# Two transformer layers on one core: weight splits, routing chain, first keys and last batch rearranged

## The reference

```python
x = layernorm(x + latent_attention(x))     # 16 heads, causal, rank 192 queries, rank 64 keys and values
x = layernorm(x + experts(x))              # 16 experts of 256-128-256, the best 2 for each token
x = layernorm(x + attention(x, Wq, Wk, Wv, Wo, bo))  # 16 query heads, 4 key heads, rotary, alibi, 30*tanh(s/30)
x = layernorm(x + x @ binarised(weight).T + bias)
```

## Time and profile before

| | |
|---|---|
| median of 3 executions | 567.59 us |
| the profiled execution, its own time | 566.75 us |
| its span, first to last instruction | 564.9 us |
| mean granted TensorE clock | 0.957 |
| TensorE busy | 508.0 us, 90% |
| VectorE busy | 394.8 us, 70% |
| ScalarE busy | 337.0 us, 60% |
| GpSimd busy | 308.7 us, 55% |
| chain that ended last, by engine | PE 68%, DVE 10%, ACT 6%, issue 5%, DMA 5%, POOL 4% |

### The profile page before, as it was taken

The page is one execution under the profiler, slowest core; times in us unless marked ns, Lnnn a source line. Parts: engine busy times, 40 slices in busy tenths (PEclk is TensorE's granted clock), DMA queues, the critical chain, the costliest instruction groups (busy, mean ns, idle before and its releaser), DMA issues.

```text
span 564.9 us, 10664 instructions
## 1 busy us (share of the span) xinstructions
PE 508.0 (90%) x3547; PEld 438.8 (78%) x3570; DVE 394.8 (70%) x840; ACT 337.0 (60%) x755; POOL 308.7 (55%) x300
## 2 busy tenths in 40 slices
PE   8889999999996995699993798999999999999982
PEld 7568888888874884486772587999999899999882
DVE  2678888888872165749753688778866995578464
ACT  5546677777765244253340587768766866686552
POOL 4846777677763024639753168766544644466210
PEclk9999999999998997789996899999999999999996
DMA  8939999900000921243575000000000000000011
GB/s 279 391 113 372 305 323 316 313 13 0 0 0 1 368 116 56 82 128 106 160 253 209 23 0 2 1 1 1 2 2 0 1 1 2 2 1 2 1 38 39
DMA packets 17582, 56.80 MB, mean 101 GB/s; under 512 B 2580, under 2 KB 12314, under 8 KB 15738
## 3 DMA queue, kind: packets, MB, share of 16 engines
q1 hardware_dynamic: 14784, 49.81, 26.0%
q0 software_dynamic: 2752, 6.40, 3.2%
HBM read 49.19 MB, written 28.45 MB: 137 GB/s over the span
## 4 chain that ended last, share of the span: by engine, by line
PE 68%; DVE 10%; ACT 6%; issue 5%; DMA 5%; POOL 4%; SPq 1%; ACTq 0%; DVEq 0%; POOLq 0%
PE bank L435 10%; PE bank L437 8%; PE bank L436 8%; PE bank L483 5%; PE bank L525 4%; PE bank L544 3%; PE bank L906 3%; PE bank L527 2%; PE bank L668 2%; PE bank L653 2%; PE bank L655 2%; PE bank L654 2%; PE bank L555 2%; DMA wqk_raw<-in_wqk 2%; PE bank L923 2%
## 5 line engine op out<-in xcount | busy, mean ns | idle before, releaser
L999 ACT ACTIVATE probs<-bank,neg_max,q_scale 128x256 f32<-128x256 f32 (+1 forms) x128 | 63.7, 507 | 39.4 <-DVE neg_max L1565 39.4
L1775 POOL TENSOR_TENSOR probs<-probs,inv_sum 128x512 f32<-128x512 f32 x64 | 51.6, 827 | 44.0 <-DVE inv_sum L1573 44.0
L1808 POOL TENSOR_TENSOR exps<-exps,tables 128x256 f32<-128x256 f32 x32 | 25.2, 787 | 77.0 <-ACT exps L1092 77.0
L1795 POOL TENSOR_TENSOR swapped<-swapped,tables 128x512 f32<-128x512 f32 x32 | 42.9, 1339 | 24.0 <-ACT swapped L1030 23.8
L1092 ACT ACTIVATE exps<-bank 128x768 f32<-128x768 f32 x32 | 25.9, 810 | 42.2 <-PE bank L635 42.2
L1405 DVE TENSOR_TENSOR q_lo<-q_sum,q_hi 128x512 fp32r<-128x512 f32 x32 | 28.0, 877 | 28.4 <-ACT q_hi L1063 28.3
L1551 DVE TENSOR_TENSOR swapped<-bank,tables 32x512 f32<-32x512 f32 x64 | 44.4, 693 | 1.4
L1767 POOL TENSOR_TENSOR qT<-qT,swapped 128x512 f32<-128x512 f32 x32 | 40.8, 1274 | 7.1 <-DVE swapped L1551 7.1
L1911 POOL DMA_INDIRECT y_rows<-y_slot,dest x31 | 30.1, 972 | 23.7 <-DVE y_slot L1743 13.8
L435 PE MATMUL bank<-x,wq_hi 128*128 128x256 f32 x128 | 39.1, 306 | 2.7 <-DVE q_sum L1392 2.6
L525 PE MATMUL bank<-keysT,qT 128*128 128x256 f32 x128 | 38.3, 381 | 0.7 <-ACT wo_full L1214 0.7
(11 more groups left out here) (264 smaller groups left out, 1801.3 us busy)
## 6 DMA issues: line engine op xcount, KB each, us to landing
slots<-in_c_unused SPq DMA_DIRECT2D x20, 1036.0 KB, 36.9
gu_all<-in_gate_up SPq DMA_DIRECT2D x4, 1024.0 KB, 8.1
xg<-slots SPq DMA_DIRECT2D x31, 129.5 KB, 2.2
wvo_raw<-in_wvo SPq DMA_DIRECT2D x1, 2560.0 KB, 21.1
dn_all<-in_down SPq DMA_DIRECT2D x1, 2048.0 KB, 8.4
wq_full<-in_Wq SPq DMA_DIRECT2D x1, 2048.0 KB, 15.7
wo_raw<-in_Wo SPq DMA_DIRECT2D x1, 2048.0 KB, 10.7
yg<-y_rows SPq DMA_DIRECT2D x4, 512.0 KB, 5.2
```

What stands on the lines that cost most here:

```text
L999: ins = act.activation(probs[:, par, h, c0:c1], bank[:, 2 * par + h, c0:c1], ACT.Exp, bias=neg_max[:, par, i:i + 1], scale=q_scale[:, b, t ...
L1775: ins = pool.tensor_tensor(some, some, inv, ALU.mult)
L1795: pool.tensor_tensor(sw, sw, sin_rows(), ALU.mult).then_inc(at1["sin_done"], 1)
```

## The change

- Routing: marks are summed by TensorE in PSUM, onto the region addresses, in place of two VectorE steps; the index and slot casts and the address step are gone. In batch 3 the two tiles are added and measured apart. The sum of variance and epsilon is left to ScalarE's bias input. 14 filler matmuls stand ahead of the last transposes.
- Splits: all eight high parts ahead of the blocks on ScalarE; key, value and four query parts on VectorE, four on GpSimd. The routing weights come after them. `gated` and `act_tok` share memory with `swapped`; `y_slot` has six buffers. SP reads the block's register ahead of its wait. The filler rows have eight kinds.
- Layer 1: keys and values of both halves ahead of the first scores; ScalarE loads the Tanh table after the first swaps; the first bias rows move from step 1 to step 7 on GpSimd, the sine of the second keys from step 1 to step 0. In the last two steps ScalarE copies the context ahead of Exp.
- Last batch: output, norm, transposes, products and statistics by tile; the bias is added by TensorE with an identity; the last tile is scaled on VectorE, the one before on ScalarE, and each is stored by its own DMA.

```diff
@@ -37,9 +37,10 @@
 W = D + 3
-KINDS = 6
+KINDS = 8
 XG = 6
-WARM = (20, 50, 18)
+YS = 6
+WARM = (20, 50, 18, 14)
@@ -458,19 +469,35 @@
         mm.then_inc(mo["logits_done"], 1)
+        if b == 0:
+            eng.wait_ge(mo["region_ready"], 1)
+        else:
+            eng.wait_ge(mo["marked"], b)
+            eng.wait_ge(mo["slots_ready"], b)
+        dst = bank[:, prefix_bank(b), 4 * E:6 * E]
+        eng.matmul(dst, ident_bf[:], region_bf[:].unsqueeze(1).broadcast_to([P, 2, E]), start=True, stop=False,
+                   skip_group_check=True)
+        for t in range(2 * b):
+            if b == 1 and t == 0:
+                eng.wait_ge(ld["alibi_in"], 48)
+            eng.matmul(dst, ones_bf, marks[:, t:t + 1, :].broadcast_to([P, 2, E]), start=False, stop=False,
+                       skip_group_check=True)
...
-        eng.wait_ge(mo["marked"], 2 * b + 1)
+        eng.wait_ge(mo["marked"], b + 1)
...
-        dst = bank[:, xT_bank(b), 4 * E:6 * E]
-        eng.matmul(dst, earlier, marks[:, 2 * b:2 * b + 2, :], start=True, stop=False, skip_group_check=True)
-        if b:
-            eng.matmul(dst, ones_bf, marks_so_far[:, b:b + 1, :].broadcast_to([P, 2, E]), start=False, stop=False,
-                       skip_group_check=True)
+        dst = bank[:, prefix_bank(b), 4 * E:6 * E]
+        eng.matmul(dst, earlier, marks[:, 2 * b:2 * b + 2, :], start=False, stop=False, skip_group_check=True)
...
@@ -491,6 +518,7 @@
         pe_prefix(eng, B - 2)
+        keep_busy(eng, WARM[3])
@@ -674,16 +703,22 @@
         if b == 0:
-            eng.wait_ge(kv["w_lo"], PAIRS + p + 1)
+            eng.wait_ge(kv["w_lo"], PAIRS // 2 + p + 1)
...
+        last = n == B * PAIRS - 1
+        if last:
+            eng.wait_ge(at1["cos_done"], B * PAIRS)
...
+            apart = last and tile == 1
+            dst = bank[:, QRY, 0:D] if apart else bank[:, Y1, tile * D:tile * D + D]
             for h in range(2):
-                mm = three_pass(eng, bank[:, Y1, tile * D:tile * D + D], c_hi[:, n % 2, h, some], c_lo[:, n % 2, h, some],
+                mm = three_pass(eng, dst, c_hi[:, n % 2, h, some], c_lo[:, n % 2, h, some],
                                 wo_hi[:, 2 * p + h, :], wo_lo[:, 2 * p + h, :],
-                                p == 0 and tile == 0 and h == 0, p == PAIRS - 1 and h == 1)
-        mm.then_inc(at1["out_done"], 1)
+                                (p == 0 and tile == 0 or apart) and h == 0, p == PAIRS - 1 and h == 1)
+            if last or tile == 1:
+                mm.then_inc(at1["out_done"], 1)
@@ -696,6 +731,34 @@
+    def pe_last_bias(eng):
+        eng.wait_ge(ld["tables_in"], 16)
+        eng.wait_ge(at1["capped"], B * PAIRS)
+        eng.wait_ge(at1["ctx_norm"], B * PAIRS)
+        for j in range(2):
+            eng.matmul(bank[:, last_z_bank(j), 0:D], ident[:], bias_rows, start=True, stop=False, skip_group_check=True)
...
@@ -712,6 +775,8 @@
         pe_values1(eng, 0, 0)
+        pe_values1(eng, 0, 1)
+        pe_keys1(eng, 0, 1)
@@ -734,10 +799,6 @@
                     pe_values1(eng, b + 1, 1)
-            if n == 0:
-                pe_values1(eng, 0, 1)
-            if n == 1:
-                pe_keys1(eng, 0, 1)
@@ -754,8 +815,9 @@
         pe_ffn(eng, 2)
-        pe_turn_x(eng, 2, B - 1)
-        pe_ffn(eng, B - 1)
+        pe_last_bias(eng)
+        pe_turn_last_x(eng)
+        pe_last_ffn(eng)
@@ -1062,26 +1119,40 @@
+    def act_last_x_hi(act, j):
+        act.wait_ge(ln["xT_done"], parts_of(2, B - 1) + j)
+        act.activation(x1[:, B - 1, 0, :, j * P:j * P + P],
+                       bank[:, last_x_bank(j), 0:D].rearrange("p (k t) -> p k t", k=KD),
+                       ACT.Copy).then_inc(ln["xT_hi_done"], 1)
...
-        for t in (2 * b, 2 * b + 1):
+        for t in (2 * b, 2 * b + 1)[0:2 if b < B - 1 else 1]:
...
+        def context_hi(n):
+            act.wait_ge(at1["ctxT_done"], n - 1)
+            if n >= 4:
+                act.wait_ge(at1["out_done"], n - 3)
+            act.activation(c_hi[:, n % 2, :, :], pair_view(bank[:, CTX, :]), ACT.Copy).then_inc(at1["c_hi"], 1)
...
+        act_swap_keys(act, 0, 0)
+        act_swap_queries(act, 0)
+        act_swap_queries(act, 1)
+        act_keys_hi(act, 0, 0)
+        act_query_hi(act, 0)
...
-        act_swap_keys(act, 0, 0)
-        act_swap_queries(act, 0)
-        act_keys_hi(act, 0, 0)
-        act_swap_queries(act, 1)
-        act_query_hi(act, 0)
+        act_values(act, 0, 0)
+        act_values(act, 0, 1)
         act_swap_queries(act, 2)
-        act_values(act, 0, 0)
@@ -1094,22 +1165,19 @@
                 act_swap_queries(act, n + 3)
+            if b < B and n + 2 >= B * PAIRS:
+                context_hi(n)
...
-            if n >= 2:
-                act.wait_ge(at1["ctxT_done"], n - 1)
-                if n >= 4:
-                    act.wait_ge(at1["out_done"], n - 3)
-                act.activation(c_hi[:, n % 2, :, :], pair_view(bank[:, CTX, :]), ACT.Copy).then_inc(at1["c_hi"], 1)
+            if n >= 2 and not (b < B and n + 2 >= B * PAIRS):
+                context_hi(n)
             if n == 0:
-                act_values(act, 0, 1)
+                act_swap_keys(act, 0, 1)
...
-                act_swap_keys(act, 0, 1)
-            if n == 2:
@@ -1239,16 +1308,15 @@
+        act.wait_ge(ld["wq1_in"], 16)
+        act.wait_ge(ln["y_done"], NT)
+        for i in range(PAIRS):
+            act.activation(chunk(wq_hi, i), chunk(wq_full, i), ACT.Copy).then_inc(kv["w_hi"], 1)
...
-            if k == 2:
-                act.wait_ge(ld["wq1_in"], 16)
-                act.wait_ge(ln["y_done"], NT)
-            if 2 <= k < 2 + PAIRS:
-                act.activation(chunk(wq_hi, k - 2), chunk(wq_full, k - 2), ACT.Copy).then_inc(kv["w_hi"], 1)
@@ -1269,29 +1337,43 @@
+        def add_y(t):
+            dve.wait_ge(ln["y_done"], t + 1)
+            dve.tensor_tensor(x_tok[:, t, :], bank[:, t % 4, 0:D], x_tok[:, t, :], ALU.add).then_inc(ln["y_read"], 1)
+        def tile_moments(t):
+            dve.wait_ge(ln["y_read"], t + 1)
+            dve.wait_ge(dve_step, counted(dve.bn_stats(bn_out[:, t, :], x_tok[:, t, :])))
+            dve.bn_aggr(moments[:, t, :], bn_out[:, t, :]).then_inc(ln["var_ready"], 1)
...
-            if b >= 1:
+            if b == B - 1:
+                add_y(2 * b)
+                tile_moments(2 * b)
                 pick(b - 1)
-            dve.wait_ge(ln["y_done"], 2 * b + 2)
-            dve.tensor_tensor(x_tok[:, two, :], y_tiles(b), x_tok[:, two, :], ALU.add).then_inc(ln["y_read"], 2)
-            dve.wait_ge(ln["y_read"], 2 * b + 2)
-            dve_statistics(dve, counted, 0, b)
+                add_y(2 * b + 1)
+                place(b - 1)
+                tile_moments(2 * b + 1)
+            else:
+                if b >= 1:
+                    pick(b - 1)
+                dve.wait_ge(ln["y_done"], 2 * b + 2)
+                dve.tensor_tensor(x_tok[:, two, :], y_tiles(b), x_tok[:, two, :], ALU.add).then_inc(ln["y_read"], 2)
+                dve.wait_ge(ln["y_read"], 2 * b + 2)
+                dve_statistics(dve, counted, 0, b)
             dve_normalise(dve, counted, 0, b)
-            if b >= 1:
+            if 1 <= b < B - 1:
...
@@ -1514,16 +1615,27 @@
         shift_of(1)
-        add_y(3)
-        statistics(2, 3)
+        first, second = NT - 2, NT - 1
+        add_y(B - 1)
+        dve.wait_ge(n2["y_read"], B)
+        tile_statistics(first)
+        dve.wait_ge(at1["out_done"], B * PAIRS + 1)
+        dve.tensor_tensor(x_tok[:, second, :], bank[:, QRY, 0:D], x_tok[:, second, :], ALU.add).then_inc(n2["y_read"], 1)
+        dve.wait_ge(n2["y_read"], B + 1)
+        tile_statistics(second)
+        normalise(2, 3)
         add_z(2)
-        normalise(2, 3)
+        last_x_lo(0)
+        last_x_lo(1)
         statistics(3, 2)
-        x_lo(2, 3)
+        add_last_z(0)
+        tile_statistics(first)
         shift_of(2)
-        add_z(3)
-        statistics(3, 3)
+        add_last_z(1)
+        tile_statistics(second)
         shift_of(3)
+        dve.tensor_scalar(x_tok[:, second, :], x_tok[:, second, :], moments[:, second, 0:1],
+                          inv_dev[:, 0, second:NT], ALU.subtract, ALU.mult).then_inc(n3["x_last"], 1)
@@ -1663,25 +1775,19 @@
                 step(dve.max_index(idx8[:, t, :], top8[:, t, :], p_tok[:, t, :]))
-            step(dve.tensor_copy(idx_f[:, two, :], idx8[:, two, 0:TOP]))
             step(dve.tensor_tensor(chosen[:, two, :, :], each(expert_ids, E),
-                                   idx_f[:, two, :].unsqueeze(3).broadcast_to([P, 2, TOP, E]), ALU.is_equal))
+                                   idx8[:, two, 0:TOP].unsqueeze(3).broadcast_to([P, 2, TOP, E]), ALU.is_equal))
...
-            dve.wait_ge(mo["marked"], 2 * b + 1)
-            step(dve.tensor_tensor(marks2[:], marks[:, 2 * b, :], marks[:, 2 * b + 1, :], ALU.add))
-            dve.tensor_tensor(marks_so_far[:, b + 1, :], marks_so_far[:, b, :], marks2[:],
```

(56 more changed lines are left out.)

125 lines of the change are left out of this document (84 added, 41 removed).

## The result

The changed kernel takes 549.82 us (median of 4 executions, 547.13 to 550.9) against 567.38 us for the kernel before (4, 564.04 to 568.15): ratio 0.968, 95% interval 0.9635 to 0.973. 549.5 had been forecast. The profiled execution is the fastest of the four: 547.13 us, span 545.3. A second measurement of it gave 550.02 (6 executions, ratio 0.9706, 0.9671 to 0.9742). One execution of experiment 4 (1268.37 us) and one of the kernel before (571.75 us) were slow ones and enter no ratio.

What follows compares the result with a forecast made beforehand. TensorE bounds the even stretches; gains lie at bends where it waits or runs at 1.2 GHz. 2.9 - 0.5 + 5.0 + 1.6 + 4.2 + 0.1 + 1.0 + 3.8 = 18.1 us gave 549.5 us, range 544.5 to 556.5.

Steps and rivals of the forecast that it cites:

- Routing: Last batch's norm and routing: earlier rows 0.6, faster clock 1.6, shorter chain 0.65, together a gain of 2.9 us.
- Splits: Expert blocks: without GpSimd's query-weight splits, seven blocks run at 1.64 us each, a gain of 5.0 us.
- the -0.5: Wait ahead of the blocks: splits laid end to end on VectorE and GpSimd delay the first gate, a loss of 0.5 us.
- End of the blocks: Last output copies and stores: six buffers instead of four bring the last issue sooner, a gain of 1.6 us.
- Start of layer 1: First steps of layer 1: idle time and lost clock go, less 1.9 us of new idle, a gain of 4.2 us.
- rival (a): Layer 1's start gains nothing net, paced by ScalarE and GpSimd; loop and tail at low ends; 556.5 us, chance 0.13.
- Epsilon: VectorE's step of adding epsilon, dropped: a gain of 0.1 us.
- End of the loop: Last context turns: ScalarE's copy put ahead of the Exp that waits for GpSimd, a gain of 1.0 us.
- Tail: Last batch's output and norm by tile, bias added by TensorE: a gain of 3.8 us.
- (b): Splits only change place and delay the first gate by 5 us instead of 0.5; 554 us, chance 0.07.
- (c): Routing fillers don't help or overrun, so the logits stay at 1.90 us; 551 us, chance 0.08.
- (d): TensorE enters the blocks at 1.2 GHz after the gather wait and stays there; 599 us, chance 0.02.

Runs made afterwards that it cites:

- experiment 4: Changed kernel with the whole order of the start of layer 1 put back as before on all four engines; median 548.80 us of three executions, ratio 0.9668.
- experiment 8: Changed kernel without the fourteen filler matmuls ahead of the last batch's transposes; median 551.15 us, ratio 0.9766.
- experiment 1: Changed kernel with the eight query-weight splits and ScalarE's eight copies back inside the expert blocks; median 554.18 us, ratio 0.9778.
- experiment 2: Changed kernel with all eight query-weight splits ahead of the blocks on VectorE, none on GpSimd; median 550.29 us.
- experiment 7: Changed kernel with four output buffers instead of six, and ScalarE's high context copies of steps 30 and 31 behind Exp again; median 552.18 us, ratio 0.9775.
- experiment 3: Changed kernel with ScalarE's root of batch 1 and Tanh table load back ahead of the first key swap; median 549.02 us, ratio 0.9689.
- experiment 6: Changed kernel with VectorE's epsilon step put back in all norms but the last batch's first and second; median 553.98 us, ratio 0.9806.
- experiment 5: Changed kernel with the last batch's tail of before: tiles as a pair, bias rows added by GpSimd, one store; median 554.18 us, ratio 0.9815.
- experiment 10: Changed kernel with the last batch's bias rows added by GpSimd instead of TensorE, tiles still apart; median 550.64 us.

## Why the prediction was right, step by step

The total was right (549.5, measured 549.82), and five of its eight terms within 0.7 us. It was right in part because one miss of 4.8 us was made up by two of 1.2 and 1.5, by smaller ones, and, in the traces, by a luckier clock; that these nearly cancel is luck.

- **Routing**, 2.9: 3.3 between the marks. The fillers' share is 1.0 (experiment 8), of 1.6 forecast; order and shorter chain together then gave some 2.3, not 1.25. The logits took 1.06 us at a granted clock of 1.00. The 0.81 of the prediction is only the part of these eight matmuls that lay on the chain of waits: in the timeline of before they take 0.96.
- **Splits**, 5.0: 5.3 (experiment 1). All 31 destination steps take 0.21 us. The turn-taking of the two engines, on which the -0.5 rested, is shown by experiment 2. The late gate was there, 0.76 us behind the end of its Silu (235.01 to 235.77), but the stage gained 0.95: before, the first up-products had run at 1.2 GHz (1.59 and 1.91 us), which the prediction missed in its own trace; after, they took 1.06 and 1.12:

```profile
239.87 1.59 PE L906 MATMUL bank<-gu_all,xgT 128*128 x4
241.68 1.91 PE L906 MATMUL bank<-gu_all,xgT 128*128 x4
```

```profile
233.64 1.06 PE L963 MATMUL bank<-gu_all,xgT 128*128 x4
234.75 1.12 PE L963 MATMUL bank<-gu_all,xgT 128*128 x4
```

- **End of the blocks**, 1.6: 1.0 (experiment 7). The error is in what comes next when a wait goes: with six buffers the last issues follow at GpSimd's own 1.27 us, not at the copies' pace.
- **Start of layer 1**, 4.2: -0.6 between the marks. This is the step that failed, and it is rival (a)'s mechanism. "So the 2.26 us idle and the 0.95 lost to the clock go" came true as written, and was worth nothing: TensorE's idle time ahead of the third queries was not on the path. The chain of waits runs mostly through ScalarE, GpSimd and VectorE there (swap, sine product, sum, high and low query, Tanh), and the moved keys and values only take away work that had filled TensorE's later waits. The term of the prediction's sum that fails is the 1.9 us of idle time left: in the new rows it is 5.69 us (17.31 busy of 23.00), where the two rows of before had 5.13 in all. From the first transposes to turn 1 TensorE is idle 7.15 of 35.67 us now and was idle 6.60 of 35.04, at nearly the same clock (0.94 and 0.95). So the idle time was moved and not won. Rows of the changed kernel's ScalarE show the price of the moved table load; from 309.23 to 315.1 it has no gap:

```profile
309.77 0.28 ACT L1075 ACTIVATE deviation<-moments,table_probe 128x2 f32<-128x2 f32 x1
310.06 1.28 ACT L1009 ACT_TABLE_LOAD   x1
311.36 0.20 ACT L1009 ACTIVATE table_probe<-ident 128x1 f32<-128x1 f32 x1
311.47 1.07 ACT L1105 ACTIVATE v_tok<-bank 128x512 f32<-128x512 f32 x2
312.56 0.59 ACT L1086 ACTIVATE swapped<-bank 64x512 f32<-64x512 f32 x1
```

  The old order costs nothing (experiment 4), which settles the 4.2. Of the new one the table load alone loses 0.9 by experiment 3; the rest of the new order would then give some 0.5 us, on one profile each. And the new order has the wait of 2.9 us told of in experiment 4. The sign that the prediction itself named, TensorE idle by more than 2 us at steps 0 to 3, was there.
- **Epsilon**, 0.1: 1.3 between the marks of the loop, of which experiment 6 shows 1.14 (turn 15 to 16), and 0.9 to 1.2 more in the tail. The trace of before held it: one row of 0.94 us in the loop among rows of 0.17, beside GpSimd. The prediction had applied that rule to the splits and, in the tail, to this very step, and not to the loop.
- **End of the loop**, 1.0: 1.1.
- **Tail**, 3.8: 4.5, of which 3.3 is the tail's own (experiment 5) and the rest for the most part the epsilon step. The 1.0 booked for GpSimd's add was this step's 1.14 beside that add; with the step gone the add holds up nothing (experiment 10). The last twelve products took 1.6 us at 2.4 GHz (538.20 to 539.80), where they had taken 2.9: the four bias products ahead of them cut TensorE's wait, which experiment 10 prices at 0.4 to 0.5. That, the prediction had not counted.
- **Clock**: 2.5 us of the traces' 19.6 are the clock's, in layer 0's attention and the start of its projection. The prediction's bound of 1% for what can be told covers it.

Rivals (b), (c) and (d) did not happen: first gate 0.76 us late, logits 1.06 us, blocks at 1.00.

## What to carry to other kernels

Idle time of the busiest engine is a price only if the chain of waits runs through it: before moving work into a gap, follow what ended the gap, and ask whether the moved work had been filling a later one. In this kernel VectorE steps of one or two columns next to a GpSimd product cost that instruction's remainder (0.17 us became 0.94, 0.21 became 1.81): search the trace for rows of one form with two durations, and take those steps out or put them elsewhere. Where two engines take turns, as with these splits, give the work to the faster one; it saves time only if that work is on the path.

## What the hardware showed that was not expected

The clock after a wait is not a fixed matter. In thirteen profiles with the same wait of 2.32 us it was down in the next products in six (four products 0.86 or 1.13 us, not 0.66) and a little later in a seventh. A wait of 2.03 or 2.04 us (turn 1, old order) was followed by 1.00 in one trace and 0.50 in another, one of 1.92 or 1.95 us ahead of turn 29 likewise, and one of 2.9 us in layer 1 (new order) by 0.50 in three profiles of six. Where one such fall can be read alone it costs 1.3 to 1.7 us, and the executions of one kernel spread over 7 us with their mean clock (0.961 to 0.978). So in this kernel a wait of TensorE of 2 us costs more than its length in some executions, and a small part must be judged by its distance in the trace with the clock beside it. That fewer waits of this kind are part of the change's gain is likely (mean clocks 0.948 to 0.967 before, 0.961 to 0.978 after) but not shown apart.
